# Keeping the gate-times-up product of an expert layer in SBUF instead of PSUM, and reading the token numbers one step sooner

## What is computed

```python
hg = jnp.einsum('nh,eih->nei', xf, Wg)          # 16 experts, 128 inner features
hu = jnp.einsum('nh,eih->nei', xf, Wu)
act = jax.nn.silu(hg) * hu
y = jnp.einsum('nei,ne,ehi->nh', act, cw, Wd)   # cw: weights of the 4 experts chosen for a token
shared = jax.nn.silu(xf @ Ws_g.T) * (xf @ Ws_u.T) @ Ws_d.T
```

## Time and profile before

| | |
|---|---|
| median of 3 runs | 2120.41 us (2116.55 to 2122.27) |
| profiled execution, its own time | 2122.27 us |
| its span, first to last instruction | 2120.5 us |
| PE busy | 2017.4 us, 95% of the span |
| DVE busy | 1664.1 us, 78% |
| ACT busy | 1413.5 us, 67% |
| POOL busy | 619.2 us, 29% |
| mean granted PE clock | 0.984 |

### The profile page before, as it was taken

The page is one execution under the profiler, slowest core; times in us unless marked ns, Lnnn a source line. Parts: engine busy times, 40 slices in busy tenths (PEclk is TensorE's granted clock), DMA queues, the critical chain, the costliest instruction groups (busy, mean ns, idle before and its releaser), DMA issues. The chain is left out here.

```text
span 2120.5 us, 44629 instructions
## 1 busy us (share of the span) xinstructions
PE 2017.4 (95%) x17981; PEld 1081.3 (51%) x17981; DVE 1664.1 (78%) x2173; ACT 1413.5 (67%) x2800; POOL 619.2 (29%) x841
## 2 busy tenths in 40 slices
PE   7999999999999999999999999999989889999997
PEld 5543333444444444344444433444444677989996
DVE  7788888999999887899999988777785765555553
ACT  5356677788888877678888888777765423444443
POOL 2011111110111111111101210313346354777876
PEclk9999999999999999999999999999998889999998
DMA  6542311122411211351111222010001525455553
GB/s 219 158 74 58 63 38 36 44 70 54 90 60 47 63 42 45 69 88 45 60 50 45 80 75 75 27 34 21 21 25 71 225 107 183 99 123 122 124 121 62
DMA packets 123937, 165.26 MB, mean 78 GB/s; under 512 B 16881, under 2 KB 99202, under 8 KB 122962
## 3 DMA queue, kind: packets, MB, share of 16 engines
q1 hardware_dynamic: 110432, 144.93, 24.4%
q0 software_dynamic: 13152, 17.45, 4.4%
q10 hardware_dynamic: 146, 0.03, 0.0%
HBM read 87.54 MB, written 75.19 MB: 77 GB/s over the span
## 5 line engine op out<-in xcount | busy, mean ns | idle before, releaser
L1046 DVE TENSOR_REDUCE mx<-S 128x2 f32<-128x1024 f32 (+3 forms) x1152 | 1277.3, 1133 | 165.3 <-PE S L913 112.8
L1016 ACT ACTIVATE prob<-ST 128x512 f32<-128x512 f32 (+3 forms) x2304 | 1167.4, 559 | 342.2 <-PE ST L934 251.8
L960 PE MATMUL O<-prob,V 128*17 128x256 f32 (+1 forms) x8704 | 670.8, 380 | 1.0 <-POOL prob L881 1.0
L913 PE MATMUL S<-K,Q 48*128 48x512 f32 (+3 forms) x2304 | 552.3, 476 | 22.9 <-DVE mx L1046 19.3
L934 PE MATMUL ST<-Q,K 49*128 49x512 f32 (+3 forms) x2304 | 477.7, 410 | 30.2 <-ACT prob L1016 25.0
L913 PEld LDWEIGHTS S<-K,Q 48*128 48x128 f32 x2304 | 215.0, 183 | 442.9 <-issue 280.1
L881 POOL TENSOR_SCALAR_AFFINE_SELECT prob<-prob 128x512 f32<-128x512 f32 x128 | 81.6, 638 | 876.0 <-ACT prob L1016 875.9
L960 PEld LDWEIGHTS O<-prob,V 128*17 128x17 f32 x8704 | 144.6, 95 | 288.6 <-issue 278.3
L934 PEld LDWEIGHTS ST<-Q,K 49*128 49x128 f32 x2304 | 217.8, 185 | 114.5 <-ACT prob L1016 91.5
L1843 PE MATMUL gate_up<-hhi,wup 128*128 128x512 f32 (+1 forms) x576 | 173.7, 369 | 1.7 <-POOL wup L1708 1.7
L1978 ACT ACTIVATE sg<-gate_up 128x512 f32<-128x512 f32 (+1 forms) x88 | 51.9, 590 | 146.8 <-PE gate_up L1843 123.6
(11 more groups left out here) (269 smaller groups left out, 1750.0 us busy)
## 6 DMA issues: line engine op xcount, KB each, us to landing
lists<-wbd SPq DMA_DIRECT2D x132, 138.0 KB, 2.4
parts<-wcut SPq DMA_DIRECT2D x108, 128.0 KB, 2.1
units<-parts SPq DMA_DIRECT2D x18, 768.0 KB, 7.0
late<-cwt SPq DMA_DIRECT2D x52, 256.0 KB
Q<-qs SPq DMA_DIRECT2D x192, 64.0 KB, 2.4
K<-ks SPq DMA_DIRECT2D x18, 512.0 KB, 9.1
xs<-lists SPq DMA_DIRECT2D x13, 552.0 KB
wraw<-in_wcat SPq DMA_DIRECT2D x54, 128.0 KB, 2.2
```

Source lines behind the costliest of these rows:

```text
L913: ins = pe.matmul(out[:, ab, 0:w], Q[g, n % QR, p, r * P:(r + 1) * P], K[G % 2][g, p, c * BW:c * BW + w], start=True, stop=not diag)
L960: ins = pe.matmul(O[32 * a:32 * a + VC, c0:c1], V[:, G, k, VC * a:VC * (a + 1)], prob[:, s % NP, a, c0:c1], start=s in FIRST and h == 0, s ...
L1016: act.activation(prob[:, s % NP, 2 * p + ab, c0:BW], ST[i % ST_BANKS][:, c0:BW], ACT.Exp).then_inc(s_exp, 1)
L1046: dve.tensor_reduce(mx[:, n % 2, a:a + step + 1:step, c], S[slot % S_RING][:, :, 0:w], AX_X, ALU.max).then_inc(s_free, 1)
```

## The change

The product of silu and up is written over `sg` in SBUF, where it was written over `hu` in PSUM. `ahi` and `alo` read it from there, so `ahi` has an SBUF source in place of a PSUM source, and `alo` has two SBUF sources, where it had one in PSUM and one in SBUF. The wait of `alo` for the product's semaphore is dropped. `tokens` of the next tile is called at `k == 0`, behind `low`, and no longer at `k == 1`, behind `alo`.

```diff
                     n = columns(items[it][0])
-                    act.activation(ahi[:, it % 2, 0:n], hu[it % 2][:, 0:n], ACT.Copy).then_inc(s_ahi, 1)
+                    act.activation(ahi[:, it % 2, 0:n], sg[:, it % 2, 0:n], ACT.Copy).then_inc(s_ahi, 1)
...
                 def product(it):
                     need("sg", s_sg, it + 1)
                     n = columns(items[it][0])
-                    up = hu[it % 2][:, 0:n]
-                    dve.tensor_tensor(up, sg[:, it % 2, 0:n], up, ALU.mult).then_inc(s_pr, 1)
+                    dve.tensor_tensor(sg[:, it % 2, 0:n], sg[:, it % 2, 0:n], hu[it % 2][:, 0:n],
+                                      ALU.mult).then_inc(s_pr, 1)
 
                 def act_low(it):
                     need("ahi", s_ahi, it + 1)
                     if it >= 2:
                         need("d", s_d, it - 1)
                     n = columns(items[it][0])
-                    need("pr", s_pr, it + 1)
-                    dve.tensor_tensor(alo[:, it % 2, 0:n], hu[it % 2][:, 0:n], ahi[:, it % 2, 0:n].bitcast(F32),
+                    dve.tensor_tensor(alo[:, it % 2, 0:n], sg[:, it % 2, 0:n], ahi[:, it % 2, 0:n].bitcast(F32),
                                       ALU.subtract).then_inc(s_act, 1)
...
                         if q < len(jobs) - 1:
                             low(q + 1)
-                    if k == 1 and q < len(jobs) - 1 and jobs[q + 1][0] == "R":
-                        tokens(jobs[q + 1][1])
+                            if jobs[q + 1][0] == "R":
+                                tokens(jobs[q + 1][1])
```

## The result

The changed kernel takes 2132.07 us (median of 15 runs) against 2121.36 us for the kernel before (15 runs): a ratio of 1.0056, 95% interval 1.0042 to 1.0070, so 0.56% slower, about 12 us by the ratio (the two medians lie 10.7 us apart). The forecast was 2122.2 us, no change, with 2115 to 2129 as its range. The profiled execution took 2134.82 us, with a span of 2133.1 us, 12.6 us more than before.

What follows compares the result with a forecast made beforehand. PE was taken to bound the routed tiles, POOL the end. 0.3 (`ahi`) + 0.3 (S jobs) + 0.8 (end) + 0.4 (`tokens`) = +1.8 us on the median of 2120.41 gave 2122.2 us, range 2115 to 2129.

Steps and rivals of the forecast that it cites:

- `tokens`: Moved cast in tiles of two halves: 1.43 us at most against 1.29 of slack; 0.1 us in each of 4, 0.4.
- a hold of up to 0.61: Cast or `alo` beside POOL's copies: kept waiting for at most the rest of one copy, 0 to 0.61 us.
- slower rival: POOL keeps the port through a whole queue of copies in the routed tiles: +14 us, 2134 us; chance 0.13.
- The rival's other half: Routed tiles: `alo` held to the queue's end, 0.46 us late for PE once in each of 13 tiles, 6.0 us.
- Product: 88 products, result to SBUF: 5 ns less each, 0.4 us over 88 items, hidden under PE's slack; counted 0.
- `ahi`: ACT's source moves to SBUF: 45 ns more, covered by slack in routed tiles, 0.3 us in S jobs; uncovered 4.0.
- `alo` by itself: 88 `alo` with two SBUF sources: no change in duration, within 0.01 us; counted 0.
- `alo` beside POOL: Held 0 to 0.61 us by a copy: nothing on PE in routed tiles, 0.3 us in S jobs, 0.8 at the end.
- one of the prediction's own signs of being wrong: Anywhere `alo` reaches 2 us; the others were PE waiting for `alo` in every tile, or for POOL's copies earlier.
- The S jobs: Jobs before the routed tiles: 0.3 us for bare `ahi` in 7 of 16 items, 0.3 for `alo` meeting POOL's sum.
- The end: Last copies, where POOL is the bound: 0.4 us at a pair, up to 0.4 at the last four; 0.8 together.
- `tokens` as a gain: Earlier cast in 18 tiles lets SP load sooner: gain 0, since SP does not wait for the cast.

Runs made afterwards that it cites:

- the product alone: Against the kernel before: product to SBUF, `ahi` and `alo` reading it there, cast left behind `alo` at `k == 1`; 2113.8 us, 1.0017.
- the move alone: Against the kernel before: only the call of `tokens` moves, product, `ahi` and `alo` as before; 2110.13 us, 0.9986.
- the copies of the change: The whole change run again (1.0078), with the cast as a two-source maximum (1.0044), or with two of its elements cast singly first (1.0061), against the kernel before.
- the run with the old product and the cast ahead of the corrections: Against the kernel before: product left in PSUM, `tokens` called before `low`; 2121.52 us, 0.9993.
- the changed kernel with its corrections in pieces: The whole change with each of the two corrections (`hlo`) in four pieces of 128 columns; 2121.24 us, 1.0046 against the kernel before.
- the one with the first item in PSUM: The whole change, but each routed tile's first product stays in PSUM and both readers take it there; 2131.45 us, 1.0046 against the kernel before.

## Why the prediction was wrong, step by step

**The step that failed is `tokens`,** and in it the sentence "a hold of up to 0.61". The cast was held 2.26 us, four copies and not the rest of one, so the sum that was put at 1.43 us at most against 1.29 of slack was really 2.26 + `ahi` 0.03 + a hold of `alo` of 0.46, 2.8 us against 1.29: 1.5 us on PE. Measured are 1.65 us in each of three tiles and 2.2 in the first, 7.2 us where the sum had 0.4. That the cast's hold is the loss in the tiles is shown: every version in which it is not held there, by an earlier or later place, by single elements, or by the old product, has its tiles back at 271.5 to 272.2 us.

The prediction had this case as its slower rival: that POOL keeps the port through a queue of copies. Its price for the tiles of two halves, 6.4 us, was near, in part by luck: it had the cast held to the end of the queue, 5.06 us behind its start, where the cast came in at 3.98, and the 0.4 us by which the queue begins later behind `alo` and the hold of the next `alo`, 0.4 to 0.5 us, which it had not counted, made up for most of that. It was rejected on one row, of a VectorE instruction that came in between two POOL instructions at 1573.6. That row is true, and it did not bear the weight: those were two instructions of 2.35 and 2.37 us with 0.08 us between them, no queue of short ones. The rival's other half, 6.0 us in the thirteen regular tiles, didn't come: `alo` there lasts 1.25 us at most where it meets a copy (1.21 at 1827.21), and PE waits for none.

**By its other steps.** Product: 5 ns less said, 10 measured at the median (686 against 696), nothing on PE, as said. `ahi`: 45 ns said, 34 and 49 measured. `alo` by itself: no change said, 691 ns before and 694 after measured. The Trainium skill ("VectorE: DVE Perf Modes", the section on the TRN2 errata) would make it 65 ns shorter, an estimate from its cycle counts; that did not show. `alo` beside POOL: in the tiles of the change held 0.56 us at most, as said; with the product alone up to 0.85, more than the 0.61 that the prediction took for the rest of one copy. Elsewhere it was more still: 1.0 us at the end (1.42 us for 256 columns), and one `alo` in the S jobs, at 1697.75, lasted 2.14 us beside a sum of POOL of 1.28 us. With that, one of the prediction's own signs of being wrong (`alo` at 2 us) did appear, but not where the loss is. The S jobs: 0.6 us said (`ahi` and POOL's sum); no loss was found: the first `ahi` of the stretch is 4.8 us later than before, the last 3.8, the third routed tile 4.4. The end: 0.8 us said, 1.0 measured; 0.6 of it by the mechanism named (0.4 us at the pair of copies, 0.2 at the last four), the rest in POOL's last sends, of which one, beside an `alo`, is 0.15 us longer. `tokens` as a gain: none, as said; the move alone is 0.9986 (0.9965 to 1.0008).

**The sum.** 7.2 + 1.0 = 8.2 us is located. The ratio says 12 us, and its interval begins at 8.9. The rest isn't settled; the copies of the change gave 1.0044 to 1.0078 with the same 278.2 to 278.7 us in the tiles, so part of it is the spread of the measurement.

**What stays open.** Why the new product turns a hold of one copy into one until the eighth. Shown: not whether the cast has one source or two, not a delay of 0.1 or 0.6 us, not its place in the queue, not one item's product alone.

In every kernel in which some `alo` of the tile reads two SBUF operands, a cast of two or four elements that asks between the first of the eight copies and 4.0 us behind it comes in at those 4.0 us (later in two first tiles: 4.5 where it asked at 2.7, and 5.1 where POOL's queue had itself been delayed by 0.4). Where none does, it comes in at the next copy, except in the run with the old product and the cast ahead of the corrections, whose long records can't be read.

The new product also changes when POOL's queue begins, 1.6 us behind the start of `alo` where it was 1.1. That distance by itself doesn't decide: in the first of these tiles it is 1.0 us in the changed kernel with its corrections in pieces, held 1.84 us, and 1.1 us in the one with the first item in PSUM, held 1.82, against 1.1 to 1.2 us in the later tiles with the old product (the run just named apart), held 0.64 at most. Not tried by themselves: ScalarE's new source, the new place of the product's result, and `alo` from PSUM in all items. A link through what an `alo` and POOL do to each other just before is not supported: in the change the send ahead of the copies is lengthened in the first of these tiles (2.04 us) and not in the others (1.54 to 1.57), with the same hold. No version beat the kernel before.

## What to carry to other kernels

A tiny instruction in the middle of a busy engine's stream can cost its own time (here 0.16 us) plus all the time that the other engine keeps it out (here up to 2.7 us). Take the whole queue of the other engine as that time, not one instruction of it, unless rows of that same queue show otherwise. Put such an instruction where its engine stands idle anyway (here ahead of the corrections: held up to 2.45 us with hardly a wait of PE), or give it a form that isn't held (here single elements). And test two edits together as well as one by one: neither half of this change costs anything in the tiles, and the two together cost 7 us there.

## What the runs showed of the hardware that was not expected

- The cast inside POOL's queue of eight copies was let in at one of two moments: at the next copy (it then lasted 0.16 to 0.64 us), or 4.0 us after the first of the eight (1.76 to 2.90 us, two first tiles later still). The Trainium skill ("SBUF — State Buffer", section "Who interferes with whom") describes the contention as an exclusive lock in which the order of issue decides who blocks. The trace agrees for `alo` in the tiles of the change, where it is held 0.56 us at most. It doesn't for the cast of 2.90 us: six copies that started after it asked went ahead of it.
- A cast of four elements or of two is held, as is a maximum with two sources; a cast of one element never was, in the same place.
- A send of POOL (indirect DMA) that begins beside an `alo` with two SBUF sources can last up to 2.06 us instead of 1.54; no send of the kernel before lasted more than 1.62.
- PE's granted clock in the unchanged attention part differed between two executions of the same code: 1.00 against 0.69 in the stretch from 1560 to 1580 us.
